# Output projection of self-attention as three f32r products instead of one fp32 product

## What is computed

```
# first layer: cross-attention to 64 context tokens, 16 heads of 64
x = x + xattn(layernorm(x), ctx)
# second layer, on n = layernorm(x)
q, k, v = n @ wq, n @ wk, n @ wv            # 16 heads of 16, causal
o = softmax(q k^T / 4, causal) @ v          # (8, 512, 256)
h = n + rmsnorm(o @ wo, attn_norm_w)        # o @ wo is the output projection
ffn = silu(h @ w1) * (h @ w3) @ w2
dense = h + rmsnorm(ffn, ff_norm_w)
# beside it a sparse path: top 2 of 8 experts for each token
x = x + dense + rmsnorm(moe(n), moe_norm_w)
```

## Time and profile before

| what | value |
|---|---|
| median of 3 runs | 1482.18 us |
| lowest, highest | 1481.14, 1485.02 us |
| span of the profiled execution, first to last instruction | 1484.5 us |
| PE busy | 1362.4 us, 92% of the span |
| DVE, POOL, ACT busy | 810.0, 600.2, 575.1 us |
| PE weight loads (beside the matmuls) | 882.2 us |
| mean granted TensorE clock | 0.976 of full speed |

### The profile page before, as it was taken

The page is one execution under the profiler, slowest core; times in us unless marked ns, Lnnn a source line. Parts: engine busy times, 40 slices in busy tenths (PEclk is TensorE's granted clock), DMA queues, the critical chain, the costliest instruction groups (busy, mean ns, idle before and its releaser), DMA issues. The chain is left out here.

```text
span 1484.5 us, 22385 instructions
## 1 busy us (share of the span) xinstructions
PE 1362.4 (92%) x7229; PEld 882.2 (59%) x7230; DVE 810.0 (55%) x1654; ACT 575.1 (39%) x1214; POOL 600.2 (40%) x1051
## 2 busy tenths in 40 slices
PE   6887899899999989998999899999999889999995
PEld 5543556666665666566656665666566346666674
DVE  2625554764585368536753675467537623333348
ACT  2231553055306521642265126503640443344446
POOL 4312353254325342634254225423542445555544
PEclk9998899999999999999999999999999899999997
DMA  6053204110501050106000500140022533322245
GB/s 213 1 153 132 86 1 121 52 30 1 142 30 30 1 156 16 30 8 160 20 15 30 141 17 15 51 121 17 1 83 74 162 107 128 129 87 85 85 186 193
DMA packets 78297, 115.39 MB, mean 78 GB/s; under 512 B 24840, under 2 KB 66208, under 8 KB 75648
## 3 DMA queue, kind: packets, MB, share of 16 engines
q1 hardware_dynamic: 67888, 79.69, 17.9%
q10 hardware_dynamic: 3840, 16.78, 4.2%
q0 software_dynamic: 6480, 17.77, 3.3%
HBM read 70.22 MB, written 43.59 MB: 77 GB/s over the span
## 5 line engine op out<-in xcount | busy, mean ns | idle before, releaser
L1540 DVE TENSOR_REDUCE nm<-ps 128x2 f32<-128x256 f32 (+3 forms) x256 | 202.5, 819 | 85.6 <-PE ps L970 79.5
L1229 ACT ACTIVATE room<-ps 128x512 f32<-128x512 f32 x320 | 179.8, 599 | 151.3 <-PE ps L996 151.1
L1051 PE MATMUL ps<-hT,w 128*128 128x512 f32 x768 | 206.5, 412 | 0.0
L703 POOL TENSOR_SCALAR_AFFINE_SELECT room<-room 128x256 f32<-128x256 f32 (+1 forms) x320 | 121.0, 390 | 136.4 <-ACT room L1229 131.7
L969 PE MATMUL ps<-room 96*128 96x128 bf16 (+3 forms) x512 | 127.9, 312 | 35.7 <-DMA room<-parts_d 17.8
L1051 PEld LDWEIGHTS ps<-hT,w 128*128 128x128 f32 x768 | 140.4, 190 | 32.1 <-DVE hT L1570 2.0
L1061 PE MATMUL ps<-w,room 128*128 128x256 f32 x512 | 137.8, 400 | 7.8 <-DVE room L1591 7.8
L1253 ACT ACTIVATE room<-ps 128x512 f32<-128x512 f32 x64 | 37.2, 593 | 277.2 <-PE ps L1051 277.2
L1087 PE MATMUL ps<-room 128*128 x284 | 135.4, 599 | 1.8 <-ACT room L1281 1.8
L920 PE MATMUL ps<-room 128*128 128x256 f32 x512 | 123.1, 384 | 2.8 <-ACT room L1190 1.8
L901 PE MATMUL ps<-room,xnT 128*128 128x512 f32 x256 | 122.0, 601 | 0.0
(11 more groups left out here) (236 smaller groups left out, 2360.1 us busy)
## 6 DMA issues: line engine op xcount, KB each, us to landing
room<-parts_d SPq DMA_DIRECT2D x48, 256.0 KB, 8.7
room<-parts_d ACTq DMA_DIRECT2D x48, 256.0 KB, 6.2
room<-xs_d SPq DMA_DIRECT2D x71, 129.0 KB
parts_d<-room SPq DMA_DIRECT2D x64, 128.0 KB, 1.8
room<-pair_d SPq DMA_DIRECT2D x8, 1024.0 KB, 7.8
room<-in_L_ffn_ew SPq DMA_DIRECT2D x24, 256.0 KB, 5.5
xin<-in_x SPq DMA_DIRECT2D x8, 512.0 KB, 11.3
parts_d<-xnT SPq DMA_DIRECT2D x32, 128.0 KB, 1.8
```

The lines of the kernel that those rows point to most:

```text
L703: done(g.affine_select(out=w, in_=w, compare_op=ALU.is_ge, fill=0.0, base=0, pattern=[[0, 2]] * (blocks - 1) + [[1, P]], channel_multiplie ...
L1051: last = mm(bank(up_banks(b, m)[i]), w[:, x, k, m * P:(m + 1) * P], hT[:, y, k, :], start=((x, y, k) == terms[0]), stop=((x, y, k) == term ...
L1229: done(fn(prob[:, u * 512:(u + 1) * 512], bank(score_bank(b) + n % 2), ACT.Exp), "b_exp")
L1540: done(v.tensor_reduce(nm[:, t, 2 * hp:2 * hp + 2], pair_ps, AX.X, ALU.max, negate=True), "a_max")
```

## The change

The output projection `o @ wo` is made as three f32r products of 256 columns into the same PSUM places: rounded oT by rounded wo, rounded oT by the rest of wo, rest of oT by rounded wo. The instructions for it:

```diff
-        wo = sb("wo", [P, KD, D])
+        wo = sb("wo", [P, 2, KD, D], F32R)
...
+        oT = over_room("oT_hi", 4096, [P, KD, S])
+        oT_lo = over_room("oT_lo", 18560, [P, KD, S])
...
+        wo_in = av[:, :].rearrange("p (k n) -> p k n", k=KD)
...
                     elif kind == "f_wo":
-                        need(pe, c, "oT_sb", 2)
+                        need(pe, c, "oT_lo", 2)
+                        if c == 0:
+                            pe.wait_ge(p0["wo_split"], 2)
                         for t in (2 * step[1], 2 * step[1] + 1):
-                            for k in range(KD):
-                                last = mm(bank((6, 7)[t // 2], D, t % 2 * D), oT[:, k, t * P:(t + 1) * P], wo[:, k, :], start=(k == 0), stop=(k == KD - 1))
+                            for x, y, k in [(x, y, k) for x, y in ((0, 0), (0, 1), (1, 0)) for k in range(KD)]:
+                                last = mm(bank((6, 7)[t // 2], D, t % 2 * D), (oT, oT_lo)[x][:, k, t * P:(t + 1) * P], wo[:, y, k, :],
+                                          start=((x, y, k) == (0, 0, 0)), stop=((x, y, k) == (1, 0, KD - 1)))
...
                     elif kind == "w_split":
+                        v.tensor_copy(wo[:, 0, :, :], wo_in).then_inc(p0["wo_split"], 1)
+                        dve.wait_ge(p0["wo_split"], 1)
+                        v.tensor_tensor(wo[:, 1, :, :], wo_in, wo[:, 0, :, :].bitcast(F32), ALU.subtract).then_inc(p0["wo_split"], 1)
                         for i, (w, src) in enumerate(zip((w1, w3), w13_in)):
...
+                    elif kind == "f_o_turn":
+                        for t2 in range(2):
+                            need(dve, c, "oT_sb", t2 + 1)
+                            cols = slice(t2 * 2 * P, (t2 + 1) * 2 * P)
+                            done(v.tensor_tensor(oT_lo[:, :, cols], bank(6 + t2).rearrange("p (k n) -> p k n", k=KD),
+                                                 oT[:, :, cols].bitcast(F32), ALU.subtract), "oT_lo")
```

More of the change, by code:

```diff
@@ L268, in xattn_ffn, with over_room @@
             pass
+        def over_room(name, at, shape):
+            with nc.sbuf_tensor(name + "_at", [P, at], F32), nc.sbuf_tensor(name, shape, F32R) as t:
+                return t
+        oT = over_room("oT_hi", 4096, [P, KD, S])
+        oT_lo = over_room("oT_lo", 18560, [P, KD, S])
         room = sb("room", [P, 28672])
@@ L652, in carry_wait, with link, rsqrt @@
                 g.tensor_tensor(spare_p[:, i:i + 1], neg_half[:, 0:1], neg_half[:, 0:1], ALU.mult)
-            def batch(b, c, end=False, only=None):
[L655 to L663, removed]
+            n_link = [0]
+            def link(ins):
+                n_link[0] += 1
+                ins.then_inc(pool_step, 1)
+                pool.wait_ge(pool_step, n_link[0])
+            def batch(b, c, end=False, only=None):
+                def rsqrt(dst, src, over, name, ve):
+                    w = src.shape[-1]
+                    link(g.tensor_tensor(ve, src, eps[:, over, 0:w], ALU.add))
+                    done(g.tensor_tensor(dst, ve, neg_half[:, 0:w], ALU.pow), name)
                 def crossed(t):
                     need(pool, b, "mv2", t + 1)
-                    rsqrt(b, rs2[:, t:t + 1], mv2[:, t, 1:2], 0, "rstd2", "pool_a", ve_a)
+                    rsqrt(rs2[:, t:t + 1], mv2[:, t, 1:2], 0, "rstd2", ve_a[:, t, 0:1])
                 for step in only or walked(b, c, end):
@@ L1362, in make_table @@
                 total = first[:, E:E + 1]
                 tile_c, expert, start, row = (t_a[:, i, :] for i in range(4))
-                chain(v.tensor_scalar(start, tile_no[:, :], 1.0, total, ALU.add, ALU.min))
-                chain(v.tensor_scalar(tile_c, start, -1.0, None, ALU.add))
+                link(v.tensor_scalar(start, tile_no[:, :], 1.0, total, ALU.add, ALU.min))
+                link(v.tensor_scalar(tile_c, start, -1.0, None, ALU.add))
                 by_expert = [P, MT, E]
                 starts = first[:, 0:E].unsqueeze(1).to_broadcast(by_expert)
-                chain(v.tensor_tensor(begun[:, :, :], tile_c.unsqueeze(2).to_broadcast(by_expert), starts, ALU.is_ge))
@@ L1371, in make_table @@
[L1371 to L1382, removed]
+                link(v.tensor_tensor(begun[:, :, :], tile_c.unsqueeze(2).to_broadcast(by_expert), starts, ALU.is_ge))
+                link(v.tensor_reduce(expert, begun[:, :, :], AX.X, ALU.add))
@@ new lines, in make_table @@
+                link(v.tensor_tensor(begun[:, :, :], begun[:, :, :], starts, ALU.mult))
+                link(v.tensor_reduce(start, begun[:, :, :], AX.X, ALU.max))
+                link(v.tensor_scalar(expert, expert, -1.0, None, ALU.add))
+                link(v.tensor_tensor(row, tile_c, start, ALU.subtract))
+                link(v.tensor_scalar(row, row, float(P), None, ALU.mult))
+                link(v.scalar_tensor_tensor(row, expert, float(REG), row, ALU.mult, ALU.add))
+                link(v.tensor_scalar(table[:, 0, :], expert, float(EW), None, ALU.mult))
@@ L1383, in make_table @@
+                link(v.tensor_scalar(start, tile_no[:, :], total, None, ALU.is_lt))
+                link(v.tensor_scalar(row, row, -float(E * REG), None, ALU.add))
+                link(v.tensor_tensor(row, row, start, ALU.mult))
                 v.tensor_scalar(table[:, 1, :], row, float(E * REG), None, ALU.add).then_inc(moe["table"], 1)
-                chain(v.tensor_scalar(start, tile_no[:, :], total, None, ALU.is_ge))
-                chain(v.tensor_tensor(start, start, tile_no[:, :], ALU.mult))
+                link(v.tensor_scalar(start, tile_no[:, :], total, None, ALU.is_ge))
@@ L1386, in make_table @@
+                link(v.tensor_tensor(start, start, tile_no[:, :], ALU.mult))
                 v.tensor_scalar(spare_off[:, :], start, float(P), None, ALU.mult).then_inc(moe["table"], 1)
             def batch(b, c, end=False, only=None):
[L1389 to L1395 removed]
                 def per_tile(x):
@@ L1416, in batch @@
                             last = v.bn_stats(st1[:, t, :], xin[:, t, :])
-                        done(last, "stats1")
-                        need(dve, n, "stats1", 1)
+                        link(last)
                         carry_wait()
```

64 lines of the change are left out of this document (26 added, 38 removed).

## The result

The changed kernel took a median of 1507.86 us over four runs (1506.15 to 1509.73), the kernel before 1481.66 us over four in the same comparison. The ratio is 1.0171, with a 95% interval of 1.0142 to 1.0200: slower by 26 us, with 1 outside the interval. In a second comparison (experiment 5) the same kernel took 1501.36 us against 1482.05, a ratio of 1.0117 (1.0086 to 1.0149): 19.3 us. The forecast was 19.5 us: the second comparison meets it, the first lies 7 us above it.

The account below looks back on a forecast made before the run. PE, busy 92% of the span, was taken as the bounding chain. Delay of `qk` 10.9 us, split 1.1 and clock 7.5 sum to 19.5 us on 1482.2: 1501.7 us, range 1491 to 1508.

Parts of the forecast that it names:

- the last walk: Projection of the walk without `norm_3`: product starts 0.8 us later, takes 0.65 less; the `xs_d` wait hides the rest, cost 0.
- The product: Projection on PE: 24 f32r records at 0.117 us replace 16 fp32 records at 0.216 us, a gain of 0.65 us a batch.
- The serial weight load: Rival at the projection: each load waits for the matmul before it, 0.217 us a record, 1520 us in all; chance 0.06.
- The wait: `f_wo 0` on PE waits for DVE's two subtractions behind `norm_3`: 2.2 us later in each of seven walks.
- The rival of a later wait: The `parts_d` transfer wait swallows the delay and the kernel gets faster, 1476.5 us; chance 0.03.
- were falls only moved: Rival: a later wait swallows half the delay and clock falls only change place, 1482 to 1487 us; chance 0.05.
- The split: Two new DVE instructions splitting wo at the end of the first walk, without cover: 1.1 us, paid once.
- The clock: PE's new 2.8 us idle stretch before the projection: five falls to half clock at 1.5 us each, 7.5 us.

Follow-up runs that it names:

- experiment 5: The changed kernel unaltered, measured again in another comparison against the kernel before: 1501.36 us, ratio 1.0117.
- Experiment 6: The kernel before with only the wait added: DVE makes both subtractions behind `norm_3`, the fp32 product waits but does not use them; 1504.68 us, ratio 1.0144.
- experiment 2: The changed kernel with `norm_3` moved behind the two subtractions in DVE's order: 1488.30 us, ratio 1.0039 to the kernel before.
- experiment 7: The changed kernel with the pair of subtractions made twice and the product waiting for the second pair: 1521.59 us, ratio 1.0252 to the kernel before.
- experiment 3: The changed kernel with 20 unused f32r matmuls filling PE's idle stretch ahead of the product in seven walks: 1495.52 us, ratio 1.0083 to the kernel before.

## Why the prediction was right, point by point

The forecast was 1501.7 us in a range of 1491 to 1508; measured were 1507.86 and 1501.36 us. The first lies 0.1 us inside the upper end, and that it lies inside is luck: the same kernel came out 6.5 us lower in the other comparison. The mechanism, a wait for the subtraction behind `norm_3` and falls of the clock at it, is what the runs show. In the sum, two small terms were wrong (the last walk, and the fall behind the split's wait, which had no term).

- **The product.** 0.117 us a record was taken from half of the 512-column stream, and 0.117 us it is; at 1.2 GHz 0.213. The stretch shrank by 0.61 us where 0.65 was said. Neither bound (0.11 and 0.216) was reached. The serial weight load is refuted by the records, each of which has a load of its own and which lie 0.117 us apart. The rule of the Trainium skill that gave this rival ("TensorE: Matmul & The Clock Gate", section "Part 3: Packing small matmuls") does not agree with the trace; the same section also lets a load go ahead of the matmuls in flight when it targets the background weight buffer, which the prediction left out and which these records do not contradict.
- **The wait.** 2.2 us was said, 2.14 measured (2.50 against 0.36). The prediction's own times give 2.25 (514.52 to 516.77); the pair begins 0.08 us before `norm_3`'s row ends and not 0.03 behind it. Experiment 6 has this wait without the rest of the change, experiment 2 takes half of it away, experiment 7 adds 1.40 us to it, and the time follows each.
- **No swallowing.** The rival of a later wait is out by experiment 7: the longer wait came out in full at the projection, and the fall of the clock with it. The six stretches between the projections, which hold the waits for `parts_d`, add up to 830.8 us before and 832.4 and 830.3 us in the two profiles of the changed kernel. Nor were falls only moved: in these stretches the clock was at half for 13.6 us before and for 20.4 and 17.0 us in the two profiles.
- **The split.** 1.1 us; the rows show 157.89 to 158.96, 1.07 us:

```profile
157.89 0.42 DVE L1515 CAST wo<-av 128x512 fp32r<-128x512 f32 x1
158.35 0.69 DVE L1517 TENSOR_TENSOR wo<-av,wo 128x512 fp32r<-128x512 f32 x1
158.96 4.48 DVE L1520 TENSOR_TENSOR w<-room,w 128x2048 fp32r<-128x2048 f32 x2
```

What the term left out is a fall of the clock. In both profiles of the changed kernel there is one behind the split's wait, from 165.5 us on, and in the kernel before none. Of the seven profiles with the split on DVE, a fall followed in the three whose wait is 2.09 to 2.26 us, and in none of the four whose wait is 1.30 to 1.99 us.

- **The last walk.** Costed at nothing, because a wait of 0.89 us for `xs_d` would hide it. This term failed. The idle stretch ahead of the product grew as said (1.41 us in the first profile, 1.57 in the second, 0.74 before), but the clock fell, so the product did not get shorter, and its cover was used up: no wait for `xs_d` is left ahead of the first transposes of the experts. From the transposes of the attention output to these it is 6.41 us in the kernel before (1199.86 to 1206.27), 7.11 in the second profile (1217.71 to 1224.82) and 7.84 in the first (1216.79 to 1224.63). The cost is 0.7 us; the first profile has 0.7 more because there the clock was already at half for the transposes of the attention output, ahead of the new idle stretch. Before, then the first profile of the changed kernel:

```profile
1199.86 1.06 PE L844 MATMUL ps<-ident,o_tok 128*128 128x128 f32 x8 [0.90 <-DVE o_tok L1564]
```

```profile
1216.79 1.88 PE L853 MATMUL ps<-ident,o_tok 128*128 128x128 f32 x8 [0.90 <-DVE o_tok L1567]
1220.08 1.22 PE L1042 MATMUL ps<-wo,oT_hi 128*128 128x256 f32 x4 [1.41 <-DVE oT_lo L1573]
...
1224.63 0.38 PE L1090 MATMUL ps<-ident,room 128*128 128x128 f32 x2
```

- **The clock.** Five falls of 1.5 us were said; the two profiles of the changed kernel have four and five at the projection, of 1.56 us each. The mechanism is shown by experiment 3, which has the delay and no falls. Its size is the loosest term: in medians the filled run lies 6 us under one result of the changed kernel and 12 under the other. The two comparisons (ratios 1.0142 to 1.0200 and 1.0086 to 1.0149) just overlap. How much of the difference is the number of falls in the runs without a profile, and how much the chip, stays open.

The forecast priced every fall at one length of 3.41 us, though one of its own rows had 6.8. A longer idle stretch does not only make the fall more frequent, it can be followed by twice the length (experiment 7).

## What to carry to other kernels

Splitting an operand adds a step between the copy out of PSUM and the product, and what it costs was decided here by the engine that makes it: look at what stands ahead of it in that engine's order, and what it waits for there. A product of rounded and remaining parts need not wait for the rest: the terms of the rounded part can run while the rest is made, which turned a loss of 20 to 26 us into a gain of 5. An idle stretch of TensorE costs its length and then, when the granted clock falls behind it, up to half of the next 3.4 us (1.56 us here); that second price is to be put into the sum of every wait that is added, small ones too.

## What the runs showed that was not expected

At the fast clock, 24 f32r records of 256 columns with a weight load each ran at 0.117 us, where 16 fp32 records had 0.216: the gain of three products over one fp32 product is there, but small (3.38 against 3.99 us with the transposes), and it is under a third of the wait that came with it (2.14 us). An idle stretch of 3.90 us was followed by 6.8 us at half clock in four walks of seven, one of 2.50 us by 3.4 us in 9 of the 14 walks with two batches of the two profiles (in 3 of 7 with fp32 records, experiment 6), and one of 1.38 us by no fall in seven. The length of the stretch alone does not decide: in the last walk, where PE had idled 0.72 and 0.90 us shortly before, a fall followed one of 1.57 to 1.58 us in all three profiles in which the clock was at full speed until then (experiments 3, 5 and 6).
